# Four of image 1's gathered tiles moved into image 0's dense steps

## The reference

```python
offset = conv2d(x, offset_w, offset_b)
# for each of 9 taps: position + offset, floor, four corners of the image, bilinear weights
vals = jax.vmap(sample_one)(x.reshape(B, C, H * W), ys, xs)
out = jnp.einsum('bckhw,ock->bohw', vals, w.reshape(w.shape[0], C, KK)) + b
# L3, f1, f2, f3 are 1 x 1 convolutions with bias of the normed x
A = jax.nn.softmax(jnp.einsum('bcn,bcm->bnm', f1, f2), axis=-1)
out = jnp.einsum('bcm,bnm->bcn', f3, A) + xf
```

## Time and profile before

| | us |
|---|---|
| median of 3 runs | 1299.03 |
| lowest and highest | 1297.82, 1301.66 |
| span of the profiled execution | 1557.5 |
| busy in it: PE, DVE, ACT, POOL | 1255.7, 993.9, 662.7, 485.1 |
| POOL, L554, 477 gathers | 461.4, 967 ns each |
| DVE, a tile's product L881, sums L891 and L895 | 1345 ns, 758 ns, 458 ns |
| DVE, block statistics L927 | 682 ns each |

### The profile page before, as it was taken

One profiled execution on the slowest core, in us unless ns is written; L12 is line 12 of the kernel. 1 busy time (PEld: TensorE's weight loads), 2 busy tenths in 40 slices (PEclk: granted clock), 3 DMA queues, 4 the chain that ended last, 5 costly groups with the idle time before them and its releaser, 6 DMA issues.

```text
span 1557.5 us, 20328 instructions
## 1 busy us (share of the span) xinstructions
PE 1255.7 (81%) x7126; PEld 508.6 (33%) x7126; DVE 993.9 (64%) x1679; ACT 662.7 (43%) x882; POOL 485.1 (31%) x537
## 2 busy tenths in 40 slices
PE   5999977387879888672587767876889999999996
PEld 1888843143423333220122222222222222222221
DVE  5899988253635544463464647665687777777772
ACT  5777766243424433111032322332346544444444
POOL 6000000746464565474655354654400000000000
PEclk9999978688988988755587779888999999999999
DMA  2655401543332331111111111111000000000000
GB/s 55 156 121 119 105 1 55 170 124 104 100 99 94 100 104 36 34 44 34 44 36 36 28 39 30 40 37 30 29 0 1 0 1 14 1 0 0 0 0 14
DMA packets 59672, 79.21 MB, mean 51 GB/s; under 512 B 12230, under 2 KB 43974, under 8 KB 59414
## 3 DMA queue, kind: packets, MB, share of 16 engines
q1 hardware_dynamic: 44342, 47.03, 11.6%
q0 software_dynamic: 15264, 31.29, 7.1%
HBM read 70.94 MB, written 7.34 MB: 50 GB/s over the span
## 4 chain that ended last, share of the span: by engine, by line
PE 58%; DVE 16%; another core or an unknown queue 12%; issue 9%; ACT 3%; SPq 1%; DVEq 1%; DMA 0%; ACTq 0%
PE psum L1971 11%; PE psum L1833 9%; PE psum L1953 9%; PE psum L1994 7%; PE psum L1718 5%; DVE maxes L1144 4%; DVE probs_and_weighted L881 3%; PE psum L1733 3%; PE psum L1668 2%; PE psum L1916 2%; PE psum L1745 2%; PE psum L1843 1%; PE psum L2000 1%; PE psum L1805 1%
## 5 line engine op out<-in xcount | busy, mean ns | idle before, releaser
L554 POOL DMA_INDIRECT tile_data<-quad_table,index_u x477 | 461.4, 967 | 626.0 <-DMA quad_table<-quad_rows_or_splits 245.2
L1144 DVE TENSOR_REDUCE maxes<-psum 128x1 f32<-128x512 f32 x512 | 331.1, 683 | 172.7 <-PE psum L1953 108.5
L1574 ACT ACTIVATE quads<-psum 128x1024 f32<-128x1024 f32 x256 | 248.2, 1021 | 329.8 <-PE psum L2000 214.8
L1971 PE MATMUL psum<-quads 128*64 128x512 f32 x1024 | 277.1, 637 | 0.0
L1833 PE MATMUL psum<-scratch,quad_rows_or_splits 128*128 128x512 f32 (+1 forms) x486 | 233.8, 626 | 33.2 <-DVE scratch L966 23.4
L1953 PE MATMUL psum<-products_or_attention 128*128 128x512 bf16 x256 | 101.5, 452 | 134.4 <-DVE maxes L1144 123.3
L1994 PE MATMUL psum<-quads,probs_and_weighted 32*128 32x512 f32 x1024 | 159.8, 696 | 2.6 <-ACT quads L1574 1.8
L1833 PEld LDWEIGHTS psum<-scratch,quad_rows_or_splits 128*128 128x128 f32 x486 | 96.3, 211 | 146.6 <-issue 126.4
L978 DVE TENSOR_TENSOR probs_and_weighted<-psum,quads 128x512 f32<-128x512 f32 (+1 forms) x81 | 50.6, 640 | 145.6 <-remote 80.2
L1433 ACT ACTIVATE vals<-psum 96x384 f32<-96x384 f32 x53 | 25.8, 487 | 222.9 <-remote 96.6
L1953 PEld LDWEIGHTS psum<-products_or_attention 128*128 (+1 forms) x256 | 20.8, 99 | 266.4 <-DVE maxes L1144 176.3
(11 more groups left out here) (227 smaller groups left out, 1464.9 us busy)
## 6 DMA issues: line engine op xcount, KB each, us to landing
products_or_attention<-positions SPq DMA_DIRECT2D x30, 576.0 KB, 8.2
products_or_attention<-bands SPq DMA_DIRECT2D x12, 768.0 KB
tile_data<-quad_table,index_u POOLq DMA_INDIRECT x477
quads<-bands SPq DMA_DIRECT2D x6, 768.0 KB
quad_table<-quad_rows_or_splits SPq DMA_DIRECT2D x4, 768.0 KB, 5.6
products_or_attention<-bands SPq DMA_DIRECT2D x4, 576.0 KB
quad_table<-quad_rows_or_splits SPq DMA_DIRECT2D x2, 640.0 KB, 7.3
products_or_attention<-positions SPq DMA_DIRECT2D x4, 288.0 KB, 7.0
```

The lines of the kernel that those rows point to most:

```text
L554: pool.indirect_dma_start(out=out[:, k * CORNERS * C:(k + 1) * CORNERS * C], out_offset=None, in_=table, in_offset=bass.IndirectOffsetOnAx ...
L1144: v.reduce_max(maxes[:, tile_of_q, block_of_k:block_of_k + 1], psum[:, FREE + c % 2, :], AXIS_X)\
L1574: act.activation(probs[:, s % 2, 2 * BLK * h:2 * BLK * (h + 1)], psum[:, SCORES + 2 * h:SCORES + 2 * h + 2, :].rearrange("p a n -> p (a n) ...
L1971: last = pe.matmul(psum[2 * C * h:2 * C * h + 2 * C, SUMS, :], f3[b][:, 4 * s + i, :], probs[:, s % 2, BLK * i:BLK * i + BLK], start=s == ...
```

## The change

Steps 1 to 25 of the dense stage now all hold a tile: 25, of which the last four are image 1's first four. The preparation has image 1's next four beside it, tiles 4 to 7 of the image, so its loop has four iterations in place of eight, and the 16 fills and 32 chunks are dealt out over four. The last 12 chunks are reduced behind the loop. The statistics of image 1's first four tiles are taken in the dense stage, and the norm's wait counts one more. The order of the gathers is the same.

```diff
-TILE_AT = {n: i for i, n in enumerate(n for n in range(1, STEPS - 1) if n not in (5, 7, 14, 21))}
+TILE_AT = {n: n - 1 for n in range(1, STEPS - 1)}
+EARLY = len(TILE_AT) - GATHERED[0]
...
-FILLS_BESIDE = [[0, 1, 2], [3, 4], [5, 6], [7, 8], [9, 10], [11, 12], [13, 14, 15], []]
-SCORED_BESIDE = [0, 4, 4, 6, 6, 6, 6, 0]
+FILLS_BESIDE = [[0, 1, 2, 3, 4], [5, 6, 7, 8, 9], [10, 11, 12, 13, 14, 15], []]
+SCORED_BESIDE = [0, 8, 12, 12]
...
+        def gathered_tile(n):
+
+            b = 0 if n < GATHERED[0] else 1
+            at = n - FIRST_OF[b]
+            return b, pair_of(at // 2), at % 2
...
                     if before is not None:
-                        finish(0, pair_of(before // 2), before % 2)
-                        if before % 4 == 3:
-                            finished_block_stats(0, (0, 0, before // 4))
+                        b, pair, u = gathered_tile(before)
+                        finish(b, pair, u)
+                        at = before - FIRST_OF[b]
+                        if at % 4 == 3:
+                            finished_block_stats(b, (0, 0, at // 4))
...
-                        weight_corners(0, pair_of(tile // 2), tile % 2)
-                        sum_corners(0, pair_of(tile // 2), tile % 2)
+                        weight_corners(*gathered_tile(tile))
+                        sum_corners(*gathered_tile(tile))
...
-                v.wait_ge(finished_stat, NBLK)
+                v.wait_ge(finished_stat, NBLK + EARLY // 4)
...
-            for t in range(2 * FIRST_MERGED):
-                if t == 0:
+            for t in range(EARLY, 2 * FIRST_MERGED):
+                if t == EARLY:
                     l3_variance()
                 weight_corners(1, pair_of(t // 2), t % 2, copied=False)
                 sum_corners(1, pair_of(t // 2), t % 2)
...
-                if t == 4:
-                    finished_block_stats(1, (0, 0, 0))
+            largest(0, first, beside_tile(2 * FIRST_MERGED - 1)[1], keys_first=True)
             take_queries(0, first)
...
-                        tile(0, pair_of(before // 2), before % 2, ahead=before + 1 < GATHERED[0])
+                        tile(*gathered_tile(before), ahead=before + 1 < len(TILE_AT))
...
-                        turn(0, pair_of(before // 2), before % 2)
+                        turn(*gathered_tile(before))
                     mix_bands(n, 2)
                     if before is not None:
-                        convolve(0, pair_of(before // 2), before % 2)
+                        convolve(*gathered_tile(before))
```

More of the change, by code:

```diff
@@ L333, in beside_tile @@
         def beside_tile(t):
-            c = sum(SCORED_BESIDE[:t])
-            return FILLS_BESIDE[t], range(c, c + SCORED_BESIDE[t])
+            at = t - EARLY
+            c = sum(SCORED_BESIDE[:at])
+            return FILLS_BESIDE[at], range(c, c + SCORED_BESIDE[at])
         FILL_AT = [(NBLK - 2, d) for d in range(1, KEY_QUADS)] + [(NBLK - 1, d) for d in range(KEY_QUADS)]
@@ L1648, in _ @@
                     take_fill(0, n)
-                if t == 3:
+                if t == 2 * FIRST_MERGED - 2:
                     l3_residual()
@@ L2085, in _ @@
                     fill(0, n)
-                if t:
+                if t > EARLY:
                     convolve(1, pair_of(t // 2), t % 2)
```

## The result

The kernel after takes 1320.2 us (median of 4 runs, 1315.8 to 1320.7), the kernel before 1300.35 (4 runs): ratio 1.0144, interval 1.0126 to 1.0162. It is 20 us slower, where 5.6 us faster was forecast and 1284 to 1304 was the range.

What follows compares the result with a forecast made beforehand. PE was taken to bound the dense steps, with nothing saturated in the preparation. Dense cost +4.4 and preparation -10 gave -5.6 us, so 1299.0 became 1293.4 us, range 1284 to 1304.

Steps and rivals of the forecast that it cites:

- late releases: Long waits put down to "remote" where gathers run, taken as the profile's own and left out; the trace exceeds the median by 258 us.
- the sum of 589: Undisturbed dense steps 260, preparation 75 and six attention blocks 254, together 589 us where the trace has 843.
- The dense cost (+4.4): Dense steps: four added tiles cost PE 1.09 us each, +4.4 us; DVE's and ACT's shares hide behind PE.
- The preparation (-10): Preparation of image 0's attention: 75 us undisturbed before, 65 after with four tiles fewer and coarser dealing, so -10 us.
- POOL's cadence: Dense steps: POOL's gathers bring tile 24 11 us late, making the stage 8 us longer; left out of the sum.
- rival B: POOL's gathers bound the dense steps: -5.6 + 8 - 3 = -0.6 us, 1298.4 us; chance 0.28.
- Four slots are filled ahead: POOL's gathers: four tiles' slots are filled ahead, and gather i+4 starts when tile i's samples are made.
- Gives back 1 to 5: Attention: POOL starts with four slots full and is never late, giving back 1 to 5 us of the dense loss.
- Rival C: Preparation: coarse fills through four banks make it serial, near 78 us; cost +7.4 us, 1306 us; chance 0.12.
- Rivals D: The median too has some late releases, part of which goes with the removed iterations: -13 us, 1286 us; chance 0.12.
- E: DVE's two sums per tile stop POOL's gathers, so a tile's nine take 12.5 us: +2.4 us, 1301.4 us; chance 0.03.
- F: Image 1's tiles aren't gathered in time for the last dense steps, so no change: 1299 us; chance 0.03.

Runs made afterwards that it cites:

- before_again: The kernel before, unchanged, profiled once more for an undisturbed trace: 1299.0 us, profiled span 1297.2 us.
- lite: The kernels before and after, each gathering 5 of a tile's 9 taps in L2: 1298.6 and 1298.4 us.
- lite_after: The kernel after with 5 of a tile's 9 gathers in L2: 1298.4 us, ratio 0.9981 to the kernel before.
- lite_before: The kernel before with 5 of a tile's 9 gathers in L2: 1298.6 us, ratio 0.9984 to the kernel before.
- coarse_prep: The kernel before's 21 tiles in the dense steps, with the kernel after's dealing of fills and chunks in the preparation: 1324.1 us, ratio 1.0173.
- lite8_after: The kernel after with 8 of a tile's 9 gathers: 1300.9 us, ratio 1.0007 to the kernel before.

## Why the prediction was wrong

**What bounds the kernel: half right.** Leaving the late releases out was right: none stands in the undisturbed traces, whose spans fit the medians, and the dense steps of before are 261 us, for which the sum said 260. But the sum of 589 closed by luck. A block of attention with tiles is 46.4 us (queries at 709.0, 755.4, 801.9 in `before_again`), not 42.3, and the three stages are 606 us there (288.5 to 894.7), not 589. What made up for it was the part ahead of the dense steps, which I took as undisturbed: it ends at 313 us in the trace of before and at 288.5 in `before_again`. The part behind 1156 us was undisturbed (401.4 us, and 402.4 there); it holds the last two blocks of image 0 as well as image 1.

**The dense cost (+4.4): right**, +3.9 by the pair of `lite` kernels, where DVE waits for no gather.

**The preparation (-10): wrong in size.** The new stage was reckoned at 65 us and is 65.0 in `lite_after`. The old one was set at 75, and is 70.7 (69.2 without gathers in the way). The walk through it was near as well: the first maximum comes 28.5 us into it there, where I said 27, and DVE idles 18.4 us, where I said 17. What I gave to the three disturbed iterations, 33.6 us, was too much: they take 28.0 in `before_again` (those of tiles 24, 25 and 28: 8.3, 10.5 and 9.2). So the change without POOL is worth 0, not -5.6: `lite_after` to `lite_before`.

**POOL's cadence: the step that decided, and it failed.** I saw half of the mechanism (rival B), priced it at 8 us less 3 given back, and kept it out of the sum; the runs show +20 us. I wrote that before, 21 tiles in 25 steps leave POOL time. They don't: POOL makes no pause in `before_again` either. So when each tile comes was fixed by the queue, whatever step it was put in. Three terms of the price were wrong:
- "Four slots are filled ahead". In the disturbed trace POOL had filled the slots and stood idle for 18.3 us, up to 338.1, until tile 0's samples were made; undisturbed DVE takes tile 0 at 304.9 while POOL fills slots until 321.3, where tile 4's first gather stands. The gather of tile 4 starts 16 us after tile 0's product begins, not when its samples are made. This is the largest error.
- 11.25 us a tile: the least distance of two gathers, not the mean. It is 11.47, 5 us over 21 tiles.
- "Gives back 1 to 5": attention takes 46.3 us a block with fewer gathers too (`lite_before`, 708.0 to 754.4), 11.6 a tile, so it had next to no wait for POOL to give back; its seven blocks are 322.8 us in the kernel after and 323.0 before.
The late tile then reads 275 + 25 x 11.47 + 1.6 = 563, against 540 due: 23 us in place of 11. The due time was off as well, and hid a part of this: 235 us lie between tile 0 and tile 24 in `lite_after`, not 227.

**The work behind the late tiles: not seen, and the other half of the loss.** I wrote that the last maxima "are in the sum". They are in a sum of DVE's work, but POOL fixes when tile 26 comes, and what is dealt behind it is added whole. The -10 was reckoned without asking when the preparation's own tiles come. Rival C looked at the coarse dealing for its waits, not for its place; in `coarse_prep` this place moves the queries by 22.8 us (642.8 against 620.05). Rivals D, E and F are out: no late releases in undisturbed runs, a pace of 11.5 and not 12.5 us a tile, and gathers of image 1 that follow those of image 0 without a pause, so that neither its table nor its indices held them up.

By the Trainium skill, "SBUF — State Buffer", section "SBUF: two separate sides", DVE can hold GpSimd off its descriptors. The mean gather in the kernel after is 0.976 us where most take 0.95, so if the rule is what lengthens the few long ones, an estimate from these means is some 0.2 us a tile here. One of them counts for more: the gather of 2.62 us at 578.24 stands among tile 26's nine, beside DVE's norm (2.58 us from 577.47), and puts off by 1.7 us the tile that sets the time. The trace agrees with the rule there, but no run separates it, and the kernel before has such a gather too (2.62 us at 553.36), so it is no part of the difference.

## What to carry to other kernels

When one queue feeds a series of tiles without a pause, write down the time at which it delivers each of them, from its real first issue and its mean pace, and ask of every tile that something waits for how much work stands behind it. Then read from the chain at which tile the time leaves the queue. Here, moving the consumers of the queue earlier brought nothing; what counted was what could be done ahead of that tile, and work dealt behind it was added to the time. Where a trace is a fifth longer than the median, its margins (which buffer was full when) are those of another execution, even if the sum of its undisturbed pieces comes out.

## What the runs showed of the hardware

- One profiled execution of the kernel before spanned 1557.5 us, another 1297.2. In the long one waits of up to 19.0 us are put down to "remote", all of them between 286 and 1156 us; in `before_again` and in the nine other traces taken since, no wait between 286 and 1000 us is. What made it was not tried.
- An indirect DMA of one index column is 0.94 to 0.95 us on POOL and 0.30 to the next, with a mean of 11.4 to 11.5 us for nine; the data were there about 1.6 us after the last of them (561.4 to 562.98).
- A ninth of POOL's gathers decides over 20 us (`lite8_after`), since already before the change its queue and DVE's schedule stood within 2 us of each other: 1.72 us of waiting at tile 28, and 0.0016 of the time by `lite_before`.
